# Two of sixteen tile transposes of the first stage: by DMA instead of by TensorE

## The reference, cut to what matters

```
x = x + tanh(g1) * ( fq(layernorm(x)) @ fq(ctx) )          # stage 1
x = x + tanh(g2) * ( y @ W_up + lora(y) ),  y = layernorm(x)   # stage 2
fq(v) = (clip(round(v / s + z), 0, 255) - z) * s
```

## Time and profile before

| | us |
|---|---|
| median of 3 executions | 959.64 |
| lowest and highest | 959.42 and 960.67 |
| profiled execution, its own time | 959.95 |
| its span on the core | 958.1 |
| TensorE busy | 936.5 |
| VectorE busy | 472.3 |
| ScalarE busy | 234.5 |

### The profile page before, as it was taken

One profiled execution on the slowest core, in us unless ns is written; L12 is line 12 of the kernel. 1 busy time (PEld: TensorE's weight loads), 2 busy tenths in 40 slices (PEclk: granted clock), 3 DMA queues, 4 the chain that ended last, 5 costly groups with the idle time before them and its releaser, 6 DMA issues.

```text
span 958.1 us, 12470 instructions
## 1 busy us (share of the span) xinstructions
PE 936.5 (98%) x5253; PEld 501.1 (52%) x5278; DVE 472.3 (49%) x1022; ACT 234.5 (24%) x196; POOL 17.1 (2%) x40
## 2 busy tenths in 40 slices
PE   3999999999999999999999999999999999999998
PEld 2444444444455555555555555555555555555554
DVE  7774757785884715343342615343342615343321
ACT  6975776777650100000000000000000000000000
POOL 0001100000000000000000000000000000000000
PEclk9999999999999999999999999999999999999999
DMA  8999987688652332222223233222223222121211
GB/s 350 422 405 406 377 318 271 227 302 290 221 152 88 111 110 44 88 44 89 44 89 88 66 111 45 88 44 88 45 88 88 61 72 44 45 45 44 44 44 44
DMA packets 77081, 135.26 MB, mean 141 GB/s; under 512 B 61936, under 2 KB 62080, under 8 KB 62720
## 3 DMA queue, kind: packets, MB, share of 16 engines
q1 hardware_dynamic: 71088, 92.74, 30.1%
q0 software_dynamic: 3488, 24.92, 6.7%
q10 hardware_dynamic: 2448, 16.78, 4.3%
HBM read 90.38 MB, written 29.37 MB: 125 GB/s over the span
## 4 chain that ended last, share of the span: by engine, by line
PE 96%; ACT 2%; DVE 1%; DMA 1%; issue 0%; SPq 0%; ACTq 0%
PE bank L1085 71%; PE bank L1003 22%; PE bank L1094 1%; PE bank L980 1%; ACT arena L414 1%; DMA rows<-in_x 1%; DVE bn L598 0%; ACT rows_T L402 0%; ACT halves L384 0%; PE bank L1077 0%; DVE arena L669 0%; SPq L282 0%; PE bank L1100 0%; DVE ln L602 0%; ACT ln L378 0%
## 5 line engine op out<-in xcount | busy, mean ns | idle before, releaser
L1085 PE MATMUL bank<-arena,rows_T 128*128 128x416 f16 (+1 forms) x3840 | 683.4, 339 | 0.0
L1085 PEld LDWEIGHTS bank<-arena,rows_T 128*128 128x128 f16 x3840 | 372.4, 97 | 304.3
L1003 PE MATMUL bank<-arena,rows_T 128*128 128x512 bf16 x999 | 222.8, 381 | 3.7 <-DVE arena L669 2.5
L1003 PEld LDWEIGHTS bank<-arena,rows_T 128*128 128x128 bf16 x1024 | 99.5, 98 | 120.6 <-issue 4.8
L783 DVE SCALAR_TENSOR_TENSOR rows<-bank,derived,rows 128x416 f32<-128x416 f32 (+2 forms) x80 | 49.8, 640 | 213.9 <-PE bank L1085 213.9
L453 ACT ACTIVATE z_stack_T<-bank 96x128 f16<-96x128 f16 x16 | 4.4, 273 | 560.1 <-PE bank L1100 560.1
L598 DVE BATCH_NORM_STATS2 bn<-rows 128x6 f32<-128x512 f32 x124 | 76.7, 678 | 5.9 <-DMA rows<-in_x 5.7
L723 DVE SCALAR_TENSOR_TENSOR route<-bank,derived,scal 128x4 f32<-128x4 f32 x16 | 3.5, 221 | 113.2 <-PE bank L1085 113.2
L659 DVE SCALAR_TENSOR_TENSOR rows<-bank,derived,rows 128x512 f32<-128x512 f32 x60 | 44.7, 748 | 25.0 <-PE bank L1003 24.6
L791 DVE SCALAR_TENSOR_TENSOR rows<-bank,z_back_scale,rows 128x512 f32<-128x512 f32 x64 | 45.1, 746 | 10.6 <-PE bank L1094 6.6
L699 DVE SCALAR_TENSOR_TENSOR halves<-normed,ln,halves 128x2048 f16<-128x2048 f32 x14 | 32.9, 2351 | 29.0 <-ACT halves L447 29.0
(11 more groups left out here) (106 smaller groups left out, 293.0 us busy)
## 6 DMA issues: line engine op xcount, KB each, us to landing
arena<-in_ctx SPq DMA_DIRECT2D x22, 1024.0 KB, 16.4
stage<-in_w SPq DMA_DIRECT2D x17, 1042.0 KB, 5.5
out<-rows ACTq DMA_DIRECT2D x15, 1024.0 KB, 3.9
h_scratch<-rows POOLq DMA_DIRECT2D x11, 1024.0 KB, 9.5
rows<-h_scratch SPq DMA_DIRECT2D x11, 1024.0 KB, 4.9
stage<-in_ctx SPq DMA_DIRECT2D x10, 1024.0 KB, 9.9
rows<-in_x POOLq DMA_DIRECT2D x10, 1024.0 KB, 9.2
normed<-in_w SPq DMA_DIRECT2D x7, 1042.0 KB, 6.5
```

The costliest lines, as they stand in the source:

```text
L1003: mm = mmul(bk, q1T[:, t % 4, kt, :], Q(b, n, kt), start=(kt == 0), stop=(kt == KT - 1 and not slow), skip_group_check=True)
L1085: mm = mmul(bank[c][:, 0:b - a], YT[:, s % 2, yh, kt, :], W(kt, wh, a, b), start=(first and kt == kts[0] and yh == 0 and wh == 0), stop=(k ...
```

## The change

The tiles 9 and 10 of stage 1 are turned by a DMA transpose of 128 x 2048 bf16, straight from `halves` into their slots of `q1T`. The two transposes are issued from SP's queue behind the first three loads of W; load 3 and the later ones follow them. Each waits for its clipped tile and for the last chunk of tile t - 4, whose slot of `q1T` it takes. TensorE no longer turns these two tiles, ScalarE no longer evacuates them (`period` skips `evac`), and whoever waited for their transposes now waits for the DMA.

```diff
+    BY_DMA = (9, 10)
+    BY_TENSOR = [t for t in range(TILES) if t not in BY_DMA]
...
+        def transposed(engine, t):
+
+            if t in BY_DMA:
+                engine.wait_ge(s_xt[t], 16)
+            else:
+                engine.wait_ge(s_tr, 2 * BY_TENSOR.index(t) + 2)
...
+            def q1_transpose(t):
+                sp.wait_ge(s_q1, t + 1)
+                sp.wait_ge(s_mm, place[(t - 4, NCH - 1)] + 1)
+                sp.dma_start_transpose(q1T[:, t % 4], q1(t)).then_inc(s_xt[t], 16)
+
+            for i in range(3):
+                load_w(i)
+            for t in BY_DMA:
+                q1_transpose(t)
+            for i in range(3, KT + 8):
                 load_w(i)
...
             def quant(t):
                 act.wait_ge(s_sb, t + 1)
                 if t >= 2:
-                    act.wait_ge(s_tr, 2 * (t - 1))
+                    transposed(act, t - 2)
...
-                evac(p + 1)
+                if p + 1 in BY_TENSOR:
+                    evac(p + 1)
...
             def half_out(t, g):
 
-                if (t, g) in BY_V:
+                if t in BY_DMA:
+                    pe.wait_ge(s_xt[t], 16)
+                elif (t, g) in BY_V:
                     pe.wait_ge(s_tv, BY_V.index((t, g)) + 1)
                 else:
-                    pe.wait_ge(s_ev, 2 * t + g + 1 - sum(1 for h in BY_V if h < (t, g)))
+                    pe.wait_ge(s_ev, 2 * BY_TENSOR.index(t) + g + 1 - sum(1 for h in BY_V if h < (t, g)))
...
                     if t >= 1:
-                        half_out(t - 1, g)
+                        half_out(BY_TENSOR[BY_TENSOR.index(t) - 1], g)
...
-                        if n == 0 and t + 1 < TILES:
+                        if n == 0 and t + 1 in BY_TENSOR:
                             transposes(t + 1)
```

More of the change, by code:

```diff
@@ L194, in build @@
         s_wc = sem("w_back_scale"); s_wr0 = sem("w_back_row_parked"); s_wr = sem("w_back_row_loaded")
-        s_dt = sem("y_transposed_by_dma")
+        s_xt = {t: sem(f"q1_transposed_by_dma{t}") for t in BY_DMA}; s_dt = sem("y_transposed_by_dma")
         s_m2 = sem("chunk2_done"); s_dl = sem("delta_done"); s_rt = sem("route_step"); s_zs = sem("z_stack_ready"); s_gl = sem("z_back_scale_ready")
@@ L302, in _ @@
                 ctx_tile(c)
-            for i in range(KT + 8):
+            def q1_transpose(t):
[7 more added lines that the diff above has]
+            for i in range(3, KT + 8):
                 load_w(i)
@@ L388, in quant @@
                     if t >= 1:
-                        act.wait_ge(s_tr, 2 * t)
+                        transposed(act, t - 1)
                     A(q1(t + 1), q1(t), ACT.Identity, accum_out=rsum[:, 0:1]).then_inc(s_rs, 1)
@@ L398, in half @@
             def half(t, g):
-                act.wait_ge(s_tr, 2 * t + g + 1)
+                act.wait_ge(s_tr, 2 * BY_TENSOR.index(t) + g + 1)
                 if t >= 4:
@@ L436, in y_high @@
                 if s == 0:
-                    act.wait_ge(s_tr, 2 * TILES)
+                    transposed(act, TILES - 1)
                 elif s <= BY_PE:
```

## The result

The changed kernel takes 976.74 us in the median of four executions (968.5 to 985.4), the kernel before 959.75. The ratio taken over fast executions alone, which leaves out the one of 985.4 us, is 1.0145 with an interval from 1.0108 to 1.0181; the two medians are 1.0177 apart. Forecast were 958.0 us. The profiled execution took 976.08 us, 16.1 more than the one of before. The scatter is new: the kernel before stays within 959.1 and 961.8 us in all its executions.

A forecast was written before the change was run, and what follows sets the result against it. TensorE alone was taken to bound the kernel: 959.95 - 1.78 spared + 0.1 wait = 958.27 us profiled, less 0.31 for the median, 957.96, say 958.0 us. The range was 957.3 to 959.3 us.

The forecast's parts named there:

- What TensorE is spared: On TensorE in stage 1: two groups of 16 transposes gone, 0.89 us each, 1.78 us in all.
- When tile 9 is needed, and when its transpose is issued: Stage 1: SP issues tile 9's transpose at 140.70 us; TensorE needs it at 155.92 us.
- When it lands: Tile 9's DMA transpose in stage 1: landing between 150.7 and 156.4 us, 157.3 with stage 2's slowest landing.
- The wait of 0.1 us: TensorE ahead of tile 9: landing taken as close to 155.5 to 156 us, so a wait of 0.1 us.
- The slower rival: TensorE waits at tile 9 until its clock drops; a wait of 2.5 us gives 962.1 us; chance 0.08.
- Its clock term: TensorE behind a long wait at tile 9: 3.5 us at the lower clock cost half of themselves, 1.7 us.
- Its condition: At tile 9: a TensorE wait of 2.0 us, a landing at 157.9 or later, brings the clock loss.
- Tile 10's ten us of cover, load 3's: Stage 1: tile 10's transpose lands by 160.0 us, needed at 169.75; load 3 of W keeps about 2 us of cover.
- That ScalarE's and VectorE's chain moves along: Stage 1's clips, W loads and row transfers all move 1.78 us earlier, keeping 0.65 us of lead at tile 15.
- The Trainium skill's rule: Tile 9's transpose at 350 to 400 GB/s: data would take 1.3 us at the upper figure and the wait vanish.

The follow-up runs named there:

- first9: Changed kernel with tile 9's transpose issued ahead of the second and third loads of W instead of behind them: 958.0 us, ratio 0.998 to the kernel before.
- only10: Changed kernel with only tile 10 transposed by DMA, tile 9 back on TensorE: 960.4 us, ratio 1.0003 to the kernel before.
- samequeue: Changed kernel with tile 7's store and tile 11's row load issued by SP behind tile 9's transpose, not by GpSimd: 958.19 us, ratio 0.9982.
- wait9: Changed kernel with both transposes held back on SP until tile 11's rows have landed: 960.54 us, ratio 1.0001 to the kernel before.
- loadbeside: Changed kernel with tile 11's row load left beside tile 9's transpose, tile 7's store waiting for its landing: 964.15 us, ratio 1.0042.
- probe2: Kernel before with GpSimd copies issued 0.4 us after stage 2's transposes, three transposes held back; executed once, 1 and 2 MB cost the transpose 7.7 and 12.5 us.
- probe: Kernel before with extra copies beside stage 2's transposes, GpSimd's issued about 2 us earlier; executed once, 1, 2 and 4 MB cost 0.8, 3.4 and 9.2 us.
- storebeside: Changed kernel with tile 7's store left beside tile 9's transpose, tile 11's row load waiting for its landing: 964.27 us, ratio 1.0058.
- only9: Changed kernel with only tile 9 transposed by DMA, behind the first three loads of W: 975.4 us, ratio 1.0169 to the kernel before.
- again: The changed kernel unaltered, run once more for a second profile: 982.51 us, ratio 1.0242 to the kernel before.

## Why the prediction was wrong, by its own steps

- *What TensorE is spared, 1.78 us:* right. 42.33 us between the two groups in first9, 28.52 in only10, and first9 and samequeue are about 2 us faster than the kernel before.
- *When tile 9 is needed, and when its transpose is issued:* right. TensorE stood from 157.45 on in a profile that is 1.35 us late, so from 156.1 (155.92 forecast); the issue began at 142.17, 0.1 us after the loads of W were issued (140.70 forecast, so 142.05 in this profile).
- *When it lands:* this step failed. Its upper end was 156.4, with the slowest landing of stage 2 157.3: the bytes of GpSimd's two transfers, then the transpose's own, each at its rate from the earlier trace rows. That supposes that two queues side by side get as much done as one after the other. They did not: 142 GB/s from 150 to 154 us and 225 through the wait, in place of 412. The landing was at 171.3, 29.1 us after the issue. I had named what the trace didn't show, small pieces beside GpSimd's large ones, and then bounded it by the rows of transfers that ran alone. Stage 2's 8.5 us was no bound for it: in the trace of the kernel before, no other queue moves a row or a tile during any of the fourteen transposes.
- *The wait of 0.1 us:* 14.0 and 21.3 us in two profiles.
- *The slower rival* named the right place, a long wait at tile 9, and the second cost, the halved clock, but had 0.08 of the chance and 2.5 us of wait. Its clock term of 1.7 us came from 3.5 us at the lower level, of which TensorE worked only 2.68; here it worked for some 5.2 us at that level, and the term was 2.6. Its condition was off too: wait9 has a wait of 2.1 us without any such cost, loadbeside one of 4.95 with 2.0.
- *Tile 10's ten us of cover, load 3's:* failed as well, by the same step, and only luck hid it. Tile 10's transpose landed at 173.3 (160.0 at the latest was forecast), 2.2 us behind the time at which tile 10 was to begin (169.75, in this profile 171.1); it cost nothing because tile 9 was later still. In only10, where it runs with the DMA engines to itself, it lands 6.1 us after its issue. Load 3 went out at 169.2 in place of 156.7, and no engine was idle for it: all were behind TensorE by then.
- *That ScalarE's and VectorE's chain moves along:* right. In first9 the clip of tile 15 ends at 229.69, the transposes start at 231.67, and nothing waits; the lead is 2.0 us, more than the 0.65 forecast. The 16.2 us a tile for the clips counts from the start of one to the end of another; from start to start it is 16.0.
- *The Trainium skill's rule* (Advanced Engine Details and Errata, X-Bar Transpose (TRN2): transposing DMAs as fast as regular ones) was set aside for the 193 GB/s of a transpose alone; beside another queue even that was far too much.

## What to carry to other kernels

A DMA transpose was cheap here only where no other queue began a large transfer while it ran (shown for GpSimd's queue, seen once for ScalarE's): give it an idle stretch of the DMA engines, or put the neighbours into its own queue behind it; holding it back until they are through works too (wait9), if the consumer can wait. Adding up bytes bounds a landing only if some row shows both queues at work together in that order. And a DMA that TensorE waits long for costs its delay and then some clock; moving one call ahead of two loads was here worth 18.7 us (976.7 to 958.0).

## What the runs showed of the hardware

- A transpose of 128 x 4096 f16 and a store of 1 MB that GpSimd issued 0.4 us behind it: 14.4 and 11.7 us to landing (probe2). With the store issued 2 us ahead of it: 7.5 and 5.8 (probe).
- In stage 1, behind two loads of W, a transpose of half the size took 20.1 us beside a load of 1 MB and 16.0 beside a store (loadbeside, storebeside), but 9.2 with both transfers behind it in its own queue (samequeue). In stage 2 a store behind it in its own queue cost nothing (6.7 us, probe).
- A starved transpose holds up the queue that issues it: 16.7 and 10.2 us of issue for tiles 9 and 10 in place of 1.9 to 2.5 (wait9, first9's tile 9, only10), 24.7 for the full size beside 4 MB in place of 4.7 to 4.9. What stands behind it in SP's program waits as long: load 3 went out at 169.2 us.
- A wait of TensorE of 2.1 us left the granted clock at 1.00 (wait9). One of 4.95 us cost 2.0 us in clock behind it (loadbeside), 5.6 us cost 2.5 (only9), 14.0 us 2.6 (the changed kernel) and 21.3 us 2.7 (again, 20.0 us for the 80 matmuls).
